# A new order for the convolutions on TensorE in a graph network kernel

## The reference

```python
for l in range(thetas.shape[0]):          # 3 layers
    xi = x[src]
    xj = x[dst]
    e = jax.nn.relu((xj - xi) @ thetas[l].T + xi @ phis[l].T)
    agg = jax.ops.segment_max(e, src, num_segments=N)
    agg = jnp.where(agg < -1e+30, 0.0, agg)
    mu = agg.mean(axis=0)
    var = agg.var(axis=0)
    x = jax.nn.relu((agg - mu) * jax.lax.rsqrt(var + BN_EPS) * gammas[l] + betas[l])
```

## Time and profile before

| | us |
|---|---|
| median of 3 runs | 1820.01 (1818.45 to 1820.69) |
| profiled execution | 1807.97 |
| its span, first to last instruction | 1806.2 |
| TensorE busy | 1096.2 (61%) |
| VectorE busy | 1252.3 (69%) |
| ScalarE busy | 994.6 (55%) |
| GpSimd busy | 973.9 (54%) |
| mean granted TensorE clock | 0.837 of full speed |

### The profile page before, as it was taken

The page is one execution under the profiler, slowest core; times in us unless marked ns, Lnnn a source line. Parts: engine busy times, 40 slices in busy tenths (PEclk is TensorE's granted clock), DMA queues, the critical chain, the costliest instruction groups (busy, mean ns, idle before and its releaser), DMA issues.

```text
span 1806.2 us, 16717 instructions
## 1 busy us (share of the span) xinstructions
PE 1096.2 (61%) x3863; PEld 564.6 (31%) x3863; DVE 1252.3 (69%) x2661; ACT 994.6 (55%) x2638; POOL 973.9 (54%) x1033
## 2 busy tenths in 40 slices
PE   0148988870016651999997699897999987000000
PEld 0023333320003331555553355453544444000000
DVE  8847777669979990455553355463666678988898
ACT  4736877764455773344443455553555453766665
POOL 1057776677767777777772777613545137630000
PEclk9999999985558785999999799998999999555555
DMA  8276899987684673688885466855866359999999
GB/s 366 106 224 228 284 347 358 365 264 240 215 308 144 221 237 104 210 265 259 262 261 148 94 181 184 173 155 127 152 137 138 87 183 307 422 402 371 365 393 370
DMA packets 177390, 436.11 MB, mean 241 GB/s; under 512 B 28804, under 2 KB 108810, under 8 KB 157324
## 3 DMA queue, kind: packets, MB, share of 16 engines
q1 hardware_dynamic: 109020, 229.52, 36.4%
q0 software_dynamic: 44800, 100.49, 21.5%
q10 hardware_dynamic: 23472, 105.03, 15.9%
HBM read 257.16 MB, written 182.32 MB: 243 GB/s over the span
## 4 chain that ended last, share of the span: by engine, by line
PE 32%; DVE 21%; DMA 21%; POOL 11%; issue 7%; ACT 6%; SPq 1%; ACTq 1%; DVEq 0%; POOLq 0%
PE ps L1262 10%; PE ps L1275 10%; DMA out<-arena 10%; DMA arena<-x 6%; POOL arena L1233 4%; PE ps L1252 3%; POOL arena L1214 3%; ACT arena L825 3%; DVE stat L786 3%; POOL slot L680 2%; PE ps L1439 2%; DVE arena L783 2%; DVE arena L1048 2%; PE ps L867 2%; DVE big L1057 2%
## 5 line engine op out<-in xcount | busy, mean ns | idle before, releaser
L1347 DVE TENSOR_TENSOR_SCAN arena<-arena,ps 128x512 f32<-128x512 f32 x150 | 191.1, 1277 | 260.2 <-PE ps L1262 235.5
L840 POOL DMA_INDIRECT arena<-x,idx x200 | 189.7, 948 | 171.4 <-DVE idx L604 91.0
L1233 POOL DMA_INDIRECT arena<-agg,slot x200 | 189.0, 945 | 171.8 <-PE ps L1252 74.1
L1262 PE MATMUL ps<-arena 128*128 128x512 f32 x600 | 277.2, 606 | 5.9 <-DVE arena L1347 5.9
L1275 PE MATMUL ps<-arena 128*128 128x512 f32 x600 | 274.1, 600 | 8.9 <-ACT arena L1317 8.9
L1214 POOL DMA_INDIRECT arena<-x,idx x200 | 189.2, 946 | 62.0 <-issue 58.8
L1544 ACT ACTIVATE ps<-arena 128x256 f32<-128x256 f32 x391 | 143.5, 367 | 102.5 <-DVE arena L1516 102.5
L825 ACT ACTIVATE arena<-arena,shift,inv 128x256 f32<-128x256 f32 (+1 forms) x311 | 156.1, 587 | 52.2 <-DVE shift L817 35.5
L1351 DVE TENSOR_TENSOR ps<-arena,ps 128x512 f32<-128x512 f32 x150 | 103.9, 695 | 105.8 <-PE ps L1275 105.8
L1317 ACT ACTIVATE arena<-big,bn_shift,bn_scale 128x512 f32<-128x512 f32 x100 | 75.9, 806 | 164.6 <-PE ps L1275 154.4
L1275 PEld LDWEIGHTS ps<-arena 128*128 128x128 f32 x600 | 115.5, 193 | 154.5 <-issue 145.1
(11 more groups left out here) (214 smaller groups left out, 2148.6 us busy)
## 6 DMA issues: line engine op xcount, KB each, us to landing
arena<-x SPq DMA_DIRECT2D x39, 1280.0 KB, 10.1
out<-arena SPq DMA_DIRECT2D x39, 1280.0 KB, 12.5
arena<-x ACTq DMA_DIRECT2D x31, 1280.0 KB, 10.7
x<-arena ACTq DMA_DIRECT2D x31, 1280.0 KB, 6.5
agg<-arena SPq DMA_DIRECT2D x50, 512.0 KB, 4.0
arena<-not_same SPq DMA_DIRECT2D x75, 256.0 KB
arena<-last_of SPq DMA_DIRECT2D x75, 256.0 KB
x_dst<-arena SPq DMA_DIRECT2D x25, 512.0 KB, 3.7
```

Source lines behind the costliest of these rows:

```text
L840: pl.indirect_dma_start(rows_in[:, par, a, g, :], None, x[:, :], bass.IndirectOffsetOnAxis(ap=idx[:, k, t * G + g:t * G + g + 1], axis=0)) ...
L1233: pl.indirect_dma_start(conv_in[:, b, 1, g, :], None, agg_dram[l - 1][:, :], bass.IndirectOffsetOnAxis(ap=slot[:, t * G + g:t * G + g + 1] ...
L1262: m = pe.matmul(far_bank[j], thp[:, l, 0, k, j * P:(j + 1) * P], far_t[:, par, k, :], start=(k == 0), stop=(k == 1))
L1347: v.tensor_tensor_scan(runmax[:, par, j, :], mask[:, tl % 2, :], far_bank[j], initial, ALU.add, ALU.max).then_inc(s_conv_scan, 1)
```

## The change

It is all in `conv_pe`, TensorE's list for the three layers. Other engines' lists are the same.

- Layer one: `turn` is called twice per tile, for the far and for the near half. A step is now turn far(t), near products(t-1), turn near(t), rows(t-2), far products(t).
- Layers two and three: far(0) now directly follows turn(0), and far(1), near(1) directly follow turn(1), ahead of turn(2). From tile 2 on the order is the old one.
- `keep_clock` is new: 4 products ahead of near(0) and 5 behind it, in layers two and three, whose result in `far_bank[0]` nobody reads. They wait for the last scan of the layer before.

```diff
-            def turn(t):
+            def turn(t, near_rows):
                 b = t % RC
-                pe.wait_ge(s_far_got[b], 64 * (ring_before(b, l, t) + 1))
-                for n in range(4 if l == 0 else 2):
+                if near_rows:
+                    pe.wait_ge(s_near_got[b], 64 * (t // RC + 1))
+                else:
+                    pe.wait_ge(s_far_got[b], 64 * (ring_before(b, l, t) + 1))
+                for n in (2, 3) if near_rows else (0, 1):
                     a, j = 1 - n // 2, n % 2
-                    if n == 2:
-                        pe.wait_ge(s_near_got[b], 64 * (t // RC + 1))
...
-            def products(t):
-                far(t)
-                if l == 0 or t:
-                    near(t)
+            def keep_clock(count):
+                pe.wait_ge(s_conv_scan, 2 * NS * l)
+                for _ in range(count):
+                    pe.matmul(far_bank[0], ident[:, :], thp[:, l, 0, :, :].rearrange("p k f -> p (k f)"), start=True, stop=True)
...
-            if l:
-                near(0)
-            in_steps([(0, turn), (1, products)] + ([(2, rows)] if l < L - 1 else []), NS)
+            if l == 0:
+                for t in range(NS):
+                    turn(t, False)
+                    if t > 0:
+                        near(t - 1)
+                    turn(t, True)
+                    if t > 1:
+                        rows(t - 2)
+                    far(t)
+                near(NS - 1)
+                rows(NS - 2)
+                rows(NS - 1)
+                return
+            keep_clock(4)
+            near(0)
+            keep_clock(5)
+            turn(0, False)
+            far(0)
+            turn(1, False)
+            far(1)
+            near(1)
+            for s in range(2, NS + 2):
+                if s < NS:
+                    turn(s, False)
+                if 2 < s <= NS:
+                    far(s - 1)
+                    near(s - 1)
+                if l < L - 1:
+                    rows(s - 2)
```

## The result

The changed kernel took a median of 1827.3 us, the kernel before 1816.45 us (20 runs each, 1813.96 to 1832.33 and 1799.17 to 1828.26). The ratio is 1.007, with a 95% interval of 1.0053 to 1.0087: slower, by 10.9 us between the medians. The forecast was +11.7 us on 1820.01.

What follows compares the result with a forecast made beforehand. TensorE was taken to bound layers one and three, GpSimd's issue most of layer two. 13.2 + 1.5 + 0 - 3.0 = +11.7 us on 1820.01 gave 1831.7 us, range 1822 to 1840 over all cases.

Steps and rivals of the forecast that it cites:

- start, near turn of tile 3 from the first turn: Layer one's start: tile 3's near turn begins at 744.3 us instead of 746.14, when its last gather lands: -1.8 us.
- 21 periods: Layer one's middle: each of 21 tile periods takes 11.07 us instead of 10.105, together +20.3 us.
- end, near turn of tile 24 to near(24)'s end: Layer one's end: less work behind the last near turn, 10.2 us instead of 15.5: -5.3 us.
- layer one: Layer one's start, 21 periods and end taken together: +13.2 us.
- masks: Last tile of layer one: masks loaded behind a store make the near sum late; +1.5 us, bounds 0 and 3.6.
- layer two: Layer two: first turns still wait for gathers, so nothing is gained; 0 us, bounds -1 and +1.
- layer three: Layer three's start: the new order brings tile 2's far products earlier; -3.0 us, bounds -1 and -3.5.
- The stall: Layer one, each tile: rows' transposes wait for ScalarE's copies of earlier rows; 1.59 us, bounds 1.4 and 2.0.
- Rival 1: Layer one: the rows' wait doesn't bite and GpSimd's gathers bind; -12.2 us there, 1804.8 us in all; 6%.
- Rival 2: Layer one: TensorE's clock swings, about 2.0 us per drop; in every third tile +14 us, 1846 us; 6%.
- Rival 3: Layer two: the mask wait, worth 7.9 us, goes as other transfers lie elsewhere; +3.8 us, 1823.8 us; 9%.
- an excess of 12 us: Whole kernel: the runs' median lies 12.0 us above the profiled execution's time, assumed to stay; 1819.7 becomes 1831.7 us.

Runs made afterwards that it cites:

- e3b: Changed kernel, with ScalarE's row copies moved between its far and near keeps in layer one; 1805.27 us, 0.9957 of the kernel before.
- e1b: Changed kernel with the new order in layer one only, later layers as before, on the faster chip; 1825.67 us, 1.0079 of the kernel before.
- e7: Changed kernel, with SyncE loading a step's masks ahead of the store of rows, in all layers; 1817.37 us, 1.0025 of the kernel before.
- e8: Changed kernel, with ScalarE's row copies between far and near keeps in layer one and masks loaded ahead of the store; 1798.11 us, 0.9911 of before.
- e5: Changed kernel without the unread products in layers two and three; 1826.7 us, 1.0083 of the kernel before.
- e1: Changed kernel with the new order in layer one only, later layers as before, on a slower chip; 2134.46 us, 0.9963 of before there.

## Why the prediction was right

Each term, as the prediction put it, against the profile after:

| term | predicted | measured |
|---|---|---|
| start, near turn of tile 3 from the first turn | -1.8 | -2.0 (36.00 for 38.01) |
| 21 periods | +20.3 (11.07 each) | +19.7 (231.94/21 = 11.045; one has 11.82, with a wait for a gather) |
| end, near turn of tile 24 to near(24)'s end | -5.3 (10.2) | -5.4 (10.13) |
| layer one | +13.2 | +12.3 |
| masks | +1.5 | +1.6 |
| layer two | 0 | +0.9 (-2.0 to tile 15, +2.8 in waits for scans) |
| layer three | -3.0 | -1.3 |
| sum | +11.7 | +13.6 (0.1 between the layers) |

- **The stall.** The rows start 2.36 us behind the near turn's start for the 2.41 worked out, 1.49 us later than without a wait; the profile's 1.32 counts from the modelled end of the turn. Between near turn and far products it is 3.26 us instead of the 3.33 that I had worked out: 0.07 less for each step. That ScalarE's order is the cause is shown by e3b (only that order changed back into idle time, and the loss became a gain), by e1b (the loss is in layer one) and by e7 (not the masks).
- **Rival 1**, rows that don't wait, is refuted for this kernel, but its price was nearly what e8 realised: forecast -12.2 us at near(24), measured -9.3 (256.48 for 265.73), by the bound that the rival named, GpSimd's issues. The rest is gathers at 1.25 us instead of 1.244 (1.0 us) and a last gather that landed later than the 3.9 us assumed.
- **Rival 2**, a swinging clock, is refuted by the 1.00 over 252 us. Two of its rows were misread: the early stage has stops of up to 3.9 us, so its clock of 0.97 is not that of stops of 1.31 us alone, and the price of a drop was 1.85 us rather than 2.0 (from the start of those far products to that of the near ones, 1173.27 to 1178.56, against 3.44).
- **Rival 3**, layer two's mask wait gone: it did not go, it came as two waits of 4.04 and 2.96 us where before one of 5.89 stood. e7 and e8 show that it goes when the masks are loaded first, and that its worth is about 7 us there.
- **Luck in layer two and in the masks.** The 0 for layer two came out as +0.9 because two misses cancel: the two waits together cost 2.8 us more than the one before, and the first 15 tiles took 2.0 less counted from the last rows. These 2.0 contain the 1.6 of the masks, which were late at the last rows as forecast but did not hold up layer two. The prediction added them as if they would.
- **The mis-sized term** is layer three. I had far(2) 17.1 us behind turn(0); it was 18.94. 1.5 of it is far(0) at a low clock (5.00 us to the start of turn(1), for 3.54 between far(1) and near(1)), where I had assumed that the unread products keep it. 0.4 lies between the starts of turn(2) and far(2), 2.64 us for the 2.2 worked out, where turn(3) waits 0.52 us for ScalarE's keeps. By e5 the new order alone gained next to nothing (193.00 for 193.12) and the unread products the rest, 1.2 us; one execution each, so this is a reading and not an interval.

What the sum was set on, an excess of 12 us of the median over the profiled execution, did not stay: it was 8.5 us over 20 runs before and 2.4 after. The difference between the medians, 10.9, is what the forecast of 11.7 should be held against. That it comes closer than the 13.6 of the three layers is partly luck: 13.6 is one pair of executions, and the profiles show nothing in the layers that would make it 2.7 less.

## What to carry to other kernels

When work is moved ahead in one engine's list, look up in the other engines' lists what it waits for, and where there: the distance that had hidden the wait may be the very thing that is taken out. Here a gap of 0.6 us per tile went and a stall of 1.5 us came, and moving two copies on an engine with idle time turned it round. Look first for the next bound as well: with gathers at 10.0 us per tile, taking the gap away could bring the period of 10.105 us down by no more than 0.1. And look at loads that queue behind stores on the same queue: two lines exchanged on SyncE took 7.8 us off layer two, in one execution each.

## What the runs showed of the hardware

- Stops of 1.32 us, one per 11 us, 22 times in a row, left TensorE at its 2.4 GHz throughout (1.00 over 252 us). Single stops for a gather in layer one did so up to 1.87 us (e3b; near products 3.60 us behind them, and so behind e8's stops of up to 1.84), while those of 1.96 and 2.28 us in e3b did not (4.69 and 4.34 us).
- Three stops of about 1.1 us within 12 us, at the start of layer three, were followed by slow far products in some executions (far(0) 5.16 us in after, 5.18 in e8) and not in others (3.70 in e7 and e3b).
- From near(24)'s end to the turn of tile 15 in layer two it took 157.2 to 158.0 us in seven of the eight profiled executions at the calm chip's times (159.5 in e3b), whether the last rows of layer one came 2.2 us behind that end (before, e7, e8) or 3.9 (after).
- The same kernel took 1814 us on one chip and 2138 and 2146 on two others. The slower ones have waits whose releaser the profile doesn't show (68.6 us in 15 waits of ScalarE at the keeps in e1); the 0.8% that layer one alone costs on the calm chip did not show on the slower one (e1 against e1b).
